# Two half-precision table pieces, four-way column-grouped totals, early fine index, evictions on ScalarE alone, in a four-layer graph kernel

## The reference, cut to what matters

```python
adj_d = where(rem, 0, adj_)             # some neighbours of crowded nodes dropped
s  = sort(where(nd, x[:, None], inf))   # per node and feature: values of the neighbours
for tau, w in zip((.25, .5, .75), (.25, .5, .25)):
    pos = tau * (nv - 1)                # nv: number of neighbours
    agg += w * (v[floor(pos)] + frac * (v[ceil(pos)] - v[floor(pos)]))
y = relu((x + agg) @ W1 + b1) @ W2 + b2
```

## Time and profile before

| | us |
|---|---|
| median of 3 runs | 3531.01 (3530.59 to 3532.71) |
| time of the profiled execution | 3535.06 |
| its span (first to last instruction) | 3533.3 |
| busy in the span: PE, DVE, ACT | 2577.4, 2814.0, 2151.4 |
| fifteen periods of layer one, from the turns of one graph to those of the next | 148.1 to 166.4 each |
| last graph's units | about 3112 to 3200 |
| remaining layers | about 3200 to 3533 |

### The profile page before, as it was taken

How to read it: one execution, slowest core, us unless ns; L and a number is a source line. 1 busy time by engine, 2 the same in 40 slices (tenths; PEclk the granted TensorE clock), 3 DMA queues, 4 the chain that set the end, 5 groups by cost and what they waited for, 6 DMA issues and landing times.

```text
span 3533.3 us, 48449 instructions
## 1 busy us (share of the span) xinstructions
PE 2577.4 (73%) x17770; PEld 1184.8 (34%) x17770; DVE 2814.0 (80%) x5341; ACT 2151.4 (61%) x3176; POOL 13.7 (0%) x24
## 2 busy tenths in 40 slices
PE   0000114788888888888888888888888888986996
PEld 0000002333333333333333333333433343333665
DVE  7999989877878778787878787878778787745676
ACT  2112433677777777777777767777777777752232
POOL 0000000000000000000000000000000000000000
PEclk6555557899998989899999999998989999987777
DMA  2002000001010101001010101010100101010011
GB/s 63 0 0 60 6 0 21 10 19 22 19 29 9 33 10 31 12 27 19 19 20 19 19 20 31 9 29 11 33 9 29 19 19 20 2 26 24 25 36 36
DMA packets 157564, 74.67 MB, mean 21 GB/s; under 512 B 125192, under 2 KB 140698, under 8 KB 157082
## 3 DMA queue, kind: packets, MB, share of 16 engines
q1 hardware_dynamic: 153210, 70.68, 8.7%
q10 hardware_dynamic: 4128, 1.05, 0.2%
HBM read 42.27 MB, written 16.83 MB: 17 GB/s over the span
## 4 chain that ended last, share of the span: by engine, by line
PE 47%; DVE 23%; ACT 19%; issue 8%; DMA 3%; SPq 0%; DVEq 0%; ACTq 0%
PE rows L621 12%; PE ring L584 8%; PE found_bank L631 6%; ACT hot L1043 6%; PE bcast L597 5%; ACT below L1008 3%; DVE keys L1306 2%; DVE keys L1305 2%; PE bcast L702 2%; PE bcast L711 2%; ACT prod L1036 2%; PE bank L873 2%; DVE delta L1347 1%; DVE delta L1345 1%; DVE perm L1349 1%
## 5 line engine op out<-in xcount | busy, mean ns | idle before, releaser
L1043 ACT ACTIVATE hot<-bcast,consts 128x1024 bf16<-128x1024 f32 x744 | 831.9, 1118 | 235.8 <-PE bcast L597 235.1
L621 PE MATMUL rows<-hot,table 128*64 128x512 bf16 x4608 | 696.9, 411 | 0.0
L584 PE MATMUL ring<-member,neigh_t 128*128 128x512 bf16 x2048 | 524.2, 400 | 46.8 <-ACT words L1000 28.7
L1036 ACT ACTIVATE prod<-rows 128x512 f32<-128x512 f32 x600 | 361.6, 603 | 119.6 <-PE rows L621 119.4
L631 PE MATMUL found_bank<-prod,consts 128*64 128x512 f32 x1536 | 416.5, 621 | 0.0
L597 PE MATMUL bcast<-idx_t,consts 32*128 32x512 f16 x1488 | 306.9, 409 | 105.7 <-ACT hot L1043 103.4
L610 PE MATMUL rows<-fine_rows,consts 32*128 32x512 bf16 x768 | 310.5, 404 | 85.3 <-DVE prod L1455 52.8
L521 PE MATMUL ring<-identb,adj_b 128*128 128x128 bf16 x256 | 35.1, 266 | 387.2 <-ACT adj_b L928 376.0
L584 PEld LDWEIGHTS ring<-member,neigh_t 128*128 128x128 bf16 x2048 | 186.6, 102 | 370.1 <-issue 111.1
L621 PEld LDWEIGHTS rows<-hot,table 128*64 128x64 bf16 x4608 | 213.9, 113 | 271.2 <-issue 203.0
L1455 DVE TENSOR_SCALAR prod<-rows 128x512 f32<-128x512 f32 x168 | 115.6, 689 | 176.9 <-PE rows L621 171.6
(11 more groups left out here) (348 smaller groups left out, 4581.1 us busy)
## 6 DMA issues: line engine op xcount, KB each, us to landing
late<-in_adj_dram SPq DMA_DIRECT2D x16, 1024.0 KB, 5.3
fine_rows<-fine_t SPq DMA_DIRECT2D x512, 24.0 KB
adjt_d<-neigh_t SPq DMA_DIRECT2D x16, 512.0 KB, 2.7
adj_l<-adjt_d SPq DMA_DIRECT2D x16, 512.0 KB, 3.5
adj_s<-adjt_d SPq DMA_DIRECT2D x16, 512.0 KB, 3.4
parts_d<-parts SPq DMA_DIRECT2D x6, 512.0 KB, 5.2
table<-parts_d SPq DMA_DIRECT2D x192, 16.0 KB, 2.2
xt_d<-keys SPq DMA_DIRECT2D x2, 1024.0 KB, 9.2
```

Of the source, the lines that this page charges most:

```text
L584: ins = mm(ring[u % 2][:, :], kept_t[:, j, P * i:P * i + P], member[:, j, n // 2, 512 * (n % 2):512 * (n % 2) + 512], start=(j == 0), stop ...
L621: ins = mm(rows[u % 2][C * h:C * h + C, :], table[:, s, GROUPS * h + g8, :], hot[:, u % HOT, h, :], start=False, stop=(s == 2), skip_group ...
L1036: run(prod[:, u % DEEP, :], rows[u % 2][:, :], ACT.Relu).then_inc(S["prod_by_act"], 1)
L1043: run(hot[:, u % HOT].rearrange(flat), spread_bank(l, u)[0][:, 0:2, :].rearrange(flat), ACT.Relu, bias=eq_bias[:, :]).then_inc(S["hot_read ...
```

## The change

1. The table has two float16 pieces in place of three bfloat16 ones: four lookup matmuls a unit in place of six, two rounds of stores to `parts_d`, eight table loads a graph in place of twelve. `hot` is float16. The sorting stage makes one piece less.
2. Totals: the matmuls have 32 output columns, and four units go to four column groups; four are issued together every fourth unit. `DEEP`, the number of `prod` buffers, is 6. The rows of `found_bank` are in another order, so `w0a_s` and `unspan` are loaded in small parts: 8 more weight loads at the start, and 32 transfers for `unspan` in place of 4.
3. `turn_idx` turns the first fine index first and the other two behind the first coarse one. `place_fine` sends one value index at a time, 64 transfers in place of 32: 16 for units 0 to 7 (by four semaphores), 16 of the same value for the other half of the values, and 32 for the rest. The last 48 have one semaphore, `later_in`, and `away` of unit 8 waits for all of them.
4. ScalarE evicts all 48 units of each graph but the last; VectorE still does the last graph's.
5. On VectorE the second `pop` stands ahead of `clear_own`.

```diff
-DEEP = 4
+DEEP = 6
-BY_VECTOR = (24, 27, 30, 33, 36, 39, 42, 45)
+ORDER = (0, 4, 1, 5, 2, 6, 3, 7)
+ROW_GROUP = (1, 1, 3, 3, 0, 0, 2, 2)
+TURN_ORDER = (K, 0, K + 1, K + 2, 1, 2, 3, 4, 5)
...
+def sum_rows(g8):
+    return 32 * (g8 // 4 + 2 * (g8 % 2))
+def by_vector(l):
+    return l == B - 1
...
+            for q in range(4):
+                for h in range(2):
+                    at = 32 * h + 16 * (q % 2)
+                    sp.dma_start(w0a_s[32 * q + 16 * h:32 * q + 16 * h + 16, :], w0a[at:at + 16, :]).then_inc(S["w_loaded"], 16)
...
             for h in range(2):
-                for to in range(2):
-                    sp.dma_start(unspan[C * to:C * to + C, 0:2 - to, h],
+                for g8 in range(GROUPS):
+                    for i in range(2):
+                        to, at = sum_rows(g8) + 16 * i + 4 * (g8 % 4), C * h + 32 * i + 4 * g8
+                        sp.dma_start(unspan[to:to + 4, :, h], span_of[at:at + 4, :]).then_inc(S["unspan_in"], 16)
...
             def place_fine(l):
-                hold(sp, S["idxT_ev"], TURNS * l + TURNS, S["sp_passed"])
+                hold(sp, S["idxT_ev"], TURNS * l + 1, S["sp_passed"])
+                for g4 in range(4):
+                    for g8 in (g4, g4 + 4):
+                        for n in range(2):
+                            fine_part(g8, n, 0, 0, 1).then_inc(fine_in[g4], 16)
+                for g8 in range(GROUPS):
+                    for n in range(2):
+                        fine_part(g8, n, 1, 0, 1).then_inc(S["later_in"], 16)
+                hold(sp, S["idxT_ev"], TURNS * l + 4, S["sp_passed"])
                 for s in range(2):
                     for g8 in range(GROUPS):
                         for n in range(2):
-                            sp.dma_start(slots_of[to + 8 * n:to + 8 * n + 8, :, s, ROW_SLOT[g8], :],
-                                         fine_t[row:row + 8, n, :, :]).then_inc(fine_in[s][g8], 16)
+                            fine_part(g8, n, s, 1, 3).then_inc(S["later_in"], 16)
...
-                    if u % 2 and u >= 3:
-                        total(l, u - 3)
-                        total(l, u - 2)
+                    if u % 4 == 1 and u >= 5:
+                        total(l, u // 4 - 1)
...
-                if u < 2 * GROUPS:
-                    pe.wait_ge(fine_in[k][g8], 32 * l + 32)
+                if u < GROUPS and u % 2 == 0:
+                    pe.wait_ge(fine_in[u // 2], 64 * l + 64)
+                if u == GROUPS:
+                    pe.wait_ge(S["later_in"], 768 * l + 768)
...
-                    for s in range(3):
-                        ins = mm(rows[u % 2][C * h:C * h + C, :], table[:, s, GROUPS * h + g8, :], hot[:, u % HOT, h, :], start=False, stop=(s == 2),
+                    for s in range(2):
+                        ins = mm(rows[u % 2][C * h:C * h + C, :], table[:, s, GROUPS * h + g8, :], hot[:, u % HOT, h, :], start=False, stop=(s == 1),
...
-                wait_evicted(pe, S["prod_by_act"], S["prod_by_dve"], l, u)
-                mm(found_bank[C * h:C * h + C, :], sum_to[:, g8, :], prod[:, u % DEEP, :], start=(u < 2), stop=(u == UNITS - 1),
-                   skip_group_check=True).then_inc(S["found_ps"], 1)
+                wait_evicted(pe, S["prod_by_act"], S["prod_by_dve"], l, 4 * m + 3)
+                for u in range(4 * m, 4 * m + 4):
+                    g8 = unit(u)[1]
+                    to = sum_rows(g8)
+                    mm(found_bank[to:to + 32, :], sum_to[:, g8 % 4, :], prod[:, u % DEEP, :], start=(m == 0), stop=(u >= UNITS - 4),
+                       skip_group_check=True).then_inc(S["found_ps"], 1)
...
-            tell("parts_ready")
-            then(tt(parts[:, 2], ordered[:, :, :], parts[:, 1], ALU.subtract))
...
                 units(l, STEP[4])
+                if t_of is not None:
+                    pop(wl, x2, x4, x8, t)
                 if p is not None:
                     clear_own(p)
```

More of the change, by code:

```diff
@@ L108, in half, with unit @@
     return [(q, g * SLOTS + q, g) for q in range(h * SLOTS // 2, (h + 1) * SLOTS // 2)]
-def by_vector(l, u):
-    return l == B - 1 or u in BY_VECTOR
+def unit(u):
+    return u // GROUPS, ORDER[u % GROUPS]
+def sum_rows(g8):
+    return 32 * (g8 // 4 + 2 * (g8 % 2))
+def by_vector(l):
+    return l == B - 1
 def wait_evicted(eng, made_a, made_v, l, u):
-    mine = [n for n in range(UNITS) if by_vector(l, n) == by_vector(l, u)]
-    if by_vector(l, u):
-        eng.wait_ge(made_v, len(BY_VECTOR) * l + mine.index(u) + 1)
+    if by_vector(l):
+        eng.wait_ge(made_v, u + 1)
     else:
-        eng.wait_ge(made_a, (UNITS - len(BY_VECTOR)) * l + mine.index(u) + 1)
+        eng.wait_ge(made_a, UNITS * l + u + 1)
 def build(nc, x_in, adj_in, mask_in, w0a, b0a, w0b, b0b, k1, gamma, beta, w2, b2,
@@ L267, in build @@
         x_t = sb("x_t", [C, N], F32)
-        hot = sb("hot", [P, HOT, 2, N], BF16)
+        hot = sb("hot", [P, HOT, 2, N], F16)
         prod = sb("prod", [P, DEEP, N], F32)
@@ L320, in build @@
         S = {n: sem(n) for n in names}
-        fine_in = [[sem(f"fine_in{s}_{g8}") for g8 in range(GROUPS)] for s in range(2)]
+        fine_in = [sem(f"fine_in{n}") for n in range(4)]
         adjs_in = [sem(f"adjs_in{q}") for q in range(SLOTS)]
@@ L463, in _ @@
             g.drain().then_inc(S["cdone"], 1)
-            g.wait_ge(S["parts_out"], 96)
+            made(g.memset(unspan[:, :, :, :], 0.0))
+            here()
+            g.drain().then_inc(S["cdone"], 1)
+            g.wait_ge(S["parts_out"], 64)
             made(g.memset(below[:, :, :, (G - 1) * C:], 1.0))
@@ L588, in spread @@
             def spread(l, u):
-                k, g8 = divmod(u, GROUPS)
+                k, g8 = unit(u)
                 at = P * (g8 % 4)
@@ L641, in dense_first @@
                 mm(dense_bank[:, :], w0a_s[:, :], sum_t[:, :], start=True, stop=False)
-                mm(dense_bank[:, :], w0a_s[0:C, :], x_t[:, :], start=False, stop=True).then_inc(S["h_ps"], 1)
+                mm(dense_bank[:, :], w0a_x[:, :], x_t[:, :], start=False, stop=True).then_inc(S["h_ps"], 1)
             def dense_second(d):
@@ L681, in turn_idx @@
                 pe.wait_ge(S["idx_ready"], b + 1)
-                for u in range(TURNS):
+                for u, k in enumerate(TURN_ORDER):
                     if u >= 2:
@@ L1026, in units @@
                         spread(l, u)
-                    if not by_vector(l, u - 2):
+                    if u >= 2 and not by_vector(l):
                         evict(l, u - 2)
@@ L1317, in _ @@
             then(ts(span_of[:, 0, :].bitcast(I32), shrink[:, :].bitcast(I32), 0x7F800000, None, ALU.bitwise_and))
+            did(ts(shrink[:, :].bitcast(I32), span_of[:, 0, :].bitcast(I32), -1.0, float(0x86000000), ALU.mult, ALU.add))
+            need(count[0])
+            then(ts(span_of[:, 0, :], span_of[:, 0, :], 2.0 ** -14, None, ALU.mult))
             tell("span_ready")
-            then(ts(shrink[:, :].bitcast(I32), span_of[:, 0, :].bitcast(I32), -1.0, float(0x7F000000), ALU.mult, ALU.add))
             for a in range(PAIRS):
@@ L1643, in norm_a @@
                 need(count[0])
-                then(ts(small[:, 14, :], moments[:, :, 1], EPS, None, ALU.add))
+                then(ts(small[:, 9, :], moments[:, :, 1], EPS, None, ALU.add))
                 tell("z_ready")
@@ L1719, in region @@
                     middles(p)
-                if t_of is not None:
-                    pop(wl, x2, x4, x8, t)
                 if p is not None:
```

112 lines of the change are left out of this document (56 added, 56 removed).

## The result

The changed kernel takes 3564.47 us (median of 5, 3555.26 to 3571.95) against 3531.01: a ratio of 1.0092, 95% interval 1.0072 to 1.0111. It is 0.9% slower where 5.4% faster was forecast, and it lies outside the range. The profiled execution has a span of 3564.3, 31.0 more than before. From the start to the first turn it is 2.7 shorter (650.1 to 647.4), the fifteen periods are 18.4 longer (mean 164.50 instead of 163.27), and what follows the last turn is 15.3 longer (449.3 instead of 434.0). A period is counted here from the first turn of one graph to that of the next, as in the earlier trace rows.

What follows compares the result with a forecast made beforehand. No engine was full: three in-order engines hand work to each other. 12.8 us a period, 192 over fifteen, less 4 in the last graph, plus 2 at the start, gave 190 off 3535.1; median 3341, range 3240 to 3437.

Steps and rivals of the forecast that it cites:

- the 1.9: At a period's start: with the first fine index already there, unit 0 gains 1.9 us.
- I take 5 as lost and 2.3 as absorbed: At unit 8's `away`: of TensorE's 7.3 us stall for the transfers, 5 lost a period, bounds 0 and 12.
- a third of the chain's share: Lookups, four matmuls for six: a third of their chain time saved, 3.3 us in `select` and 5.3 in `region`.
- the 2 for the cold clock behind the eviction stall: In `region`: the cold clock following TensorE's 3.7 us stop for VectorE goes, worth 2 us a period.
- The totals: Four column groups side by side: half the totals' chain time saved, 2.1 us in `select` and 4.3 in `region`.
- counted 0: `pop` ahead of `clear_own` only fills VectorE's 2.1 us wait for the adjacency store; counted 0.
- 3.7 + 2 - 4.8: Evictions in `region`: TensorE's 3.7 us stop and 2 of cold clock saved, 4.8 charged for ScalarE's eight evictions.
- I take 4 slower: Last graph: unit 8 is 21 us late, 40 units gain 17; 4 slower, between 3 faster and 8 slower.
- The sum for a unit, 1.10: Last graph: a unit costing 1.53 us would cost 0.32 + 0.56 + 0.22 = 1.10.
- The rivals: Gate not binding 0.2 (3250 us), ScalarE pacing or totals only in pairs 0.24 (3437), slower 0.03, no change 0.02.
- The slower case: ScalarE's idle time doesn't shrink, so its 4.8 us of evictions add to each period: 3603 us, chance 0.03.
- if less than 4.8 of the 41 goes: Test for the slower outcome: less than 4.8 of ScalarE's 41 us idle time a period goes.

Runs made afterwards that it cites:

- e1: The changed kernel with the gate split: unit 8 waits for the second 16 transfers, unit 16 for the last 32; 3401.5 us, ratio 0.9621.
- e15: The changed kernel with 30 throwaway matmuls of 128 rows by 128 columns ahead of the gate's wait at unit 8; 3529.5 us, ratio 1.0002.
- e2: The kernel before with only the new turn order, the 64 transfers and the one gate at unit 8; 3620.3 us, ratio 1.0255.
- e5: The kernel before with only the new turn order, the 64 transfers and the split gate; 3526.0 us, ratio 0.9983.
- e13: The kernel before with the table's third piece left out, four lookup matmuls a unit; 3456.2 us, ratio 0.9784.
- e4: The changed kernel with the split gate and six lookup matmuls a unit, the second piece added twice; 3402.3 us, ratio 0.9633.
- e12: The changed kernel with its one gate and six lookup matmuls a unit, the second piece added twice; 3537.6 us, ratio 1.0025.
- after: The changed kernel itself, with its one gate, against the kernel before; 3564.5 us, ratio 1.0092.
- e6: The changed kernel with split gate and six lookups, as e4, and each total issued twice; 3484.7 us, ratio 0.9870.
- e9: The kernel before with only `pop` moved ahead of `clear_own` on VectorE; 3478.0 us, ratio 0.9847.
- e14: The kernel before with the eight evictions a period moved from VectorE to ScalarE; 3458.8 us, ratio 0.9796.
- e7: The split-gate kernel e1 with `pop` back in its old, later place; 3392.7 us, ratio 0.9617.
- e3: The changed kernel with the split gate and eight evictions a period given back to VectorE; 3394.4 us, ratio 0.9613.
- e8: The kernel e3 with the last 32 transfers waited for in two halves, at units 16 and 24; 3384.8 us, ratio 0.9583.
- e11: The changed kernel with 24 throwaway matmuls of the shape of `away` ahead of the gate's wait; 3571.0 us, ratio 1.0124.

## Why the prediction was wrong

The sum had 192 us off in the fifteen periods; they grew by 18. The 210 us between split into two terms: the gate cost 10.5 a period where 5 was charged (82 us), and without it the period gained 9.3 (163.3 to 154.0, e1) where 17.8 was credited (128 us). The tail missed by 11 more.

**Right.** Four totals run side by side: eight records in 1.07 at the full clock. Four lookups take 0.63. SP's pitch is 45.19 / 64 = 0.706, inside 0.635 to 0.728; TensorE's stall at unit 8 is 7.5 for 7.3 forecast (the sum has a slip, 2172.3 - 1.9 - 2.5 is 2167.9, which makes it 7.1). Both its ends came later than forecast, unit 8 at 43.9 behind the turn for 42.7 and the last transfer at 51.4 for 50.0, so that it fits so closely is partly luck. Unit 0 starts 13.4 behind the turn in that period, 15.5 before, so the 1.9 are there. The start gave 2.7 for 2. An unchanged pitch, the 0.728 of the earlier trace rows, holds for half of them: over the sixteen graphs the 32 transfers of two rows come 0.73 to 0.77 apart and the 32 of one row 0.67 to 0.70.

**The gate: "I take 5 as lost and 2.3 as absorbed".** Nothing is absorbed. The wait alone is (136.8 - 30.2) / 15 = 7.1 a period, a cold restart adds 2.5 (e15), and 0.9 is left for what queues behind. The step that failed was that "VectorE has most of one tile in hand" covers part of the delay. It had one, and worked on it until 2022.2, 5.6 beyond the end of TensorE's wait. But its next sums stand behind more than the gate, and VectorE waits for them even without a stall: 63.0 us in thirty waits in e1, of 2.6 at most, so that a delay of TensorE there goes through whole. With the stall it is 202.3, and one wait a period is about 11 (waits and groups of the changed kernel, then the group in e1):

```profile
...
PE rows L642 <- DMA fine_rows<-fine_t: 136.8, 16, 30.2
...
```

```profile
...
L1511 DVE TENSOR_SCALAR picked<-cnt,above 128x960 bf16<-128x960 f16 x192 | 78.6, 466 | 213.9 <-PE bcast L736 202.3
...
```

```profile
...
L1513 DVE TENSOR_SCALAR picked<-cnt,above 128x960 bf16<-128x960 f16 x192 | 78.6, 466 | 74.6 <-PE bcast L738 63.0 <-ACT cnt L1035 4.4 <-DVE x_all L1686 3.3
...
```

In the old kernel the same gate costs 5.5 (e2, e5), near the 5 that I charged. The stall itself is shorter there, (104.6 - 24.4) / 15 = 5.3, and units 20 to 32 give 2.0 of the loss back (39.7 to 37.7); in the new kernel no stretch gives any back. I had taken the price of the gate as if the rest of the change had not been made. The waits of e2:

```profile
...
PE rows L623 <- DMA fine_rows<-fine_t: 104.6, 16, 24.4
...
```

**The lookups: "a third of the chain's share".** The term was 8.6. Alone in the old kernel it is 4.8 (e13), in the new one nothing (e4 against e1), and with the gate it is negative (e12). A share of the chain is time at today's clock with today's neighbours. Where TensorE got less to do it had more gaps, and its granted clock in units 20 to 32 went from 0.87 to 0.77 (e1) and 0.64 (after) in the periods shown, and to 0.74 and 0.71 over fifteen. The sum had the clock only as something to win, the 2 for the cold clock behind the eviction stall; that TensorE might stay cold longer stood among the signs of being wrong, without a price. That the clock is what takes it is shown for units 20 to 32 by e4 and e12, where more matmuls give a higher clock and less time (34.7 for 36.0, and 34.8 for 37.0); elsewhere six lookups cost e4 little, 0.7 in units 0 to 8 and 0.5 in units 32 to 47. In units 0 to 8 of e1, at the full clock, ScalarE is busy 25.4 of 30.2 and TensorE waits 4.3 for its hot rows, so shorter lookups have less to win there; that part is read from the waits, not tested.

**The totals** were sized well: 6.4, measured 5.2 (e6 against e4).

**Evictions and `pop`: "counted 0", and 3.7 + 2 - 4.8.** Alone in the old kernel `pop` early gives 4.0 a period (e9) and the evictions 5.0 (e14), and both remove the same 52.8 us of waiting. I saw that wait in the eviction term and VectorE's wait for the store in the `pop` term, and did not see that one causes the other. In the new kernel neither adds to the other: `pop` early brings nothing (e7), and the evictions on ScalarE cost 0.8 a period in the profiles, which the medians can't tell from nothing (e3). No run shows the 2 of that sum: behind the stall lookups and totals took 1.50 and 1.92 for 0.85 and 1.03, and e14, which is without the stall, gains 5.0 a period in all. The parts' gains alone (1.4, 4.8, 4.0, 5.0, and 5.2 for the totals) add to 20.4, and together they give 9.3.

**The last graph: "I take 4 slower".** It is 15.3. Unit 8 stands 40.2 behind unit 0, 49.6 behind the turn (47.5 forecast). The 40 units behind it gained 71.3 - 61.5 = 9.8, not 17: the windows of the two stretches have TensorE's busy time down by 12.4 (69.2 to 56.8), at a clock of 0.94 for 0.98, and its idle time up by 2.6, for the dense part's steps stand between those units and wait for other engines. The sum for a unit, 1.10, knew nothing of them. SP's loads behind the 64 transfers, "needed only in `region`, 30 us later", are hidden in the periods, and in the last graph as long as the units are later still: no wait for `x_t` stands in the changed kernel or in e1, but with four gates TensorE waits 9.9 for it (e8).

**The rivals.** None was it. The slower case had the right sign, at 0.03, and by its own test ("if less than 4.8 of the 41 goes") it holds: ScalarE's idle time went from 41 to 39 in the period shown. But the test doesn't tell its mechanism from others, and the mechanism is not the cause: giving the evictions back changes the time by 0.2% (e3), while splitting the gate moves it by 163 us (e1).

## What to carry to other kernels

Before one semaphore replaces many, list which instruction reads what each transfer brings: a gate at the earliest reader waits for the latest data, and here that, not the number of transfers, cost 163 us; a second semaphore, waited for eight units earlier than the other, gave it back and made the change 3.8% faster than before. A term "fewer matmuls times their time" takes the clock as unchanged, and here the clock of a stretch fell from 0.87 to 0.74 with the work (e4, e1), and four lookups took 0.63 at 1.00 and 1.07 at 0.50: look at the granted clock of the stretch, and at what else would have gaps in it. Gains of parts that touch one wait did not add here (4.0 and 5.0 a period alone, e9 and e14, both by the same 52.8 us of waiting); find for each wait in the rows what delays its releaser, and price the wait once.

## What the runs showed of the hardware

TensorE's granted clock fell to half (1.00 to 0.50) while it streamed matmuls without a gap, when these were 32x128 ones in bf16, 24 in 7.61 us (e11), and stayed at 1.00 with 128x128 ones in float16, 30 in 6.65 us (e15), in all sixteen graphs of each profile. Six lookups a unit instead of four raised the granted clock of the whole span from 0.806 to 0.846 and of units 20 to 32 from 0.74 to 0.87, at the same time (e1, e4). Four column groups of 128x32 in fp32 run side by side: their eight records take 1.07 (e15), where four records in two groups of 64 take 1.03. SP issues small transfers inside the chip 0.67 to 0.70 apart when they have one row a partition, and 0.73 to 0.77 apart when they have two (after).
